# A recommendation kernel: pair products over all 128 rows, dense layers of all samples first, last tile in four units of 32 samples

## The reference, cut to what matters

```python
emb = emb_tables[arange(26)[:, None], x_cat]            # one 64-number row per sample and field
dense_embed = price[:, None] @ Wp + bp                  # a 27th row of 64
feats = concatenate([emb, dense_embed[:, None, :]], 1)  # 2048 x 27 x 64
gram = einsum('bid,bjd->bij', feats, feats)             # all pairs of the 27 rows, per sample
interactions = gram[:, _IU, _JU]                        # 351 pairs
h = relu(dense_embed @ W1 + b1)                         # 64 -> 128
dense_out = relu(h @ W2 + b2)                           # 128 -> 64
t = relu(concatenate([interactions, dense_out], 1) @ Wt1 + bt1)   # 415 -> 256
out = (t @ Wt2 + bt2)[:, 0]
```

## Time and profile before

| what | value |
|---|---|
| time, three runs | 541.97 us median (541.65 to 544.13) |
| the profiled execution | 542.15 us, its span 540.3 us |
| POOL busy | 393.8 us (73%), 416 gathers |
| PE busy | 246.3 us (46%) |
| ACT busy | 169.1 us (31%) |
| DVE busy | 145.4 us (27%) |
| mean granted TensorE clock | 0.70 |

### The profile page before, as it was taken

How to read it: one execution, slowest core, us unless ns; L and a number is a source line. 1 busy time by engine, 2 the same in 40 slices (tenths; PEclk the granted TensorE clock), 3 DMA queues, 4 the chain that set the end, 5 groups by cost and what they waited for, 6 DMA issues and landing times.

```text
span 540.3 us, 4362 instructions
## 1 busy us (share of the span) xinstructions
PE 246.3 (46%) x1496; PEld 177.9 (33%) x1496; DVE 145.4 (27%) x358; ACT 169.1 (31%) x405; POOL 393.8 (73%) x425
## 2 busy tenths in 40 slices
PE   0118033240569515134249733315136960565775
PEld 0105033240534304133234423305134440544654
DVE  3003233040331504123040331503233051333353
ACT  0124323041241604223042440503224052243563
POOL 6777777777777777777777777777777777777750
PEclk9999665555659856555577975755555985669798
DMA  6233333333323333333333333333332333332210
GB/s 187 26 26 27 26 28 27 26 27 27 26 27 27 26 27 28 26 26 27 26 29 26 27 27 26 27 27 27 26 27 26 26 28 26 26 28 27 28 22 2
DMA packets 14360, 16.26 MB, mean 30 GB/s; under 512 B 7169, under 2 KB 7425, under 8 KB 14209
## 3 DMA queue, kind: packets, MB, share of 16 engines
q0 software_dynamic: 13312, 13.66, 30.9%
q1 hardware_dynamic: 578, 2.19, 1.1%
q10 hardware_dynamic: 448, 0.14, 0.1%
HBM read 15.95 MB, written 0.01 MB: 30 GB/s over the span
## 4 chain that ended last, share of the span: by engine, by line
POOL 68%; issue 26%; DMA 2%; PE 2%; ACT 1%; DVE 0%; POOLq 0%
POOL gathered L200 68%; DMA gathered<-in_table,row_idx 2%; PE ps_mlp L487 1%; ACT gram L141 1%; PE ps_trans L419 1%; DMA raw_idx<-in_x_cat 0%; POOLq L50 0%; PE ps_gram L456 0%; PE ps_mlp L479 0%; PE ps_mlp L495 0%; DVE feats L166 0%; DVE top L368 0%; ACT scores L279 0%; DVE row_idx L339 0%; DVE wrapped L332 0%
## 5 line engine op out<-in xcount | busy, mean ns | idle before, releaser
L200 POOL DMA_INDIRECT gathered<-in_table,row_idx x416 | 392.7, 944 | 128.0 <-issue 125.9
L419 PE MATMUL ps_trans<-ident,gathered 128*128 128x128 f32 x208 | 45.4, 381 | 223.0 <-DMA gathered<-in_table,row_idx 223.0
L456 PE MATMUL ps_gram<-feats 64*128 64x128 f32 x1024 | 105.2, 384 | 61.0 <-ACT gram L141 30.2
L141 ACT COPY gram<-ps_gram 32x112 f32<-32x112 f32 (+1 forms) x272 | 97.2, 357 | 108.1 <-PE ps_gram L456 105.2
L141 DVE COPY gram<-ps_gram 32x112 f32<-32x112 f32 (+1 forms) x272 | 96.6, 355 | 116.8 <-PE ps_gram L456 113.5
L456 PEld LDWEIGHTS ps_gram<-feats 64*128 64x128 f32 x1024 | 96.9, 286 | 75.4 <-issue 52.6
L419 PEld LDWEIGHTS ps_trans<-ident,gathered 128*128 128x128 f32 x208 | 35.0, 198 | 236.3 <-issue 234.9
L151 ACT COPY feats<-ps_trans 64x448 f32<-64x448 f32 (+1 forms) x60 | 34.1, 569 | 195.4 <-PE ps_trans L419 195.0
L151 DVE COPY feats<-ps_trans 64x448 f32<-64x448 f32 (+1 forms) x60 | 36.8, 613 | 203.3 <-PE ps_trans L419 202.7
L487 PE MATMUL ps_mlp<-gram,wt1p_sb 128*128 128x512 f32 (+2 forms) x168 | 60.2, 520 | 2.9 <-ACT gram L141 2.9
L487 PEld LDWEIGHTS ps_mlp<-gram,wt1p_sb 128*128 128x128 f32 x168 | 32.6, 228 | 32.6 <-issue 28.0
(11 more groups left out here) (24 smaller groups left out, 33.5 us busy)
## 6 DMA issues: line engine op xcount, KB each, us to landing
gathered<-in_table,row_idx POOLq DMA_INDIRECT x416, 3.3
price_bc<-in_price SPq DMA_DIRECT2D x1, 1024.0 KB, 5.2
wt1p_sb<-in_wt_pairs SPq DMA_DIRECT2D x1, 896.0 KB, 7.8
raw_idx<-in_x_cat SPq DMA_DIRECT2D x1, 195.0 KB, 2.7
w_sb<-in_w ACTq DMA_DIRECT2D x2, 32.0 KB, 4.8
wt1d_sb<-in_wt_dense ACTq DMA_DIRECT2D x1, 64.0 KB, 7.7
raw_idx<-in_x_cat SPq DMA_DIRECT2D x1, 13.0 KB, 1.8
consts_sb<-in_consts ACTq DMA_DIRECT2D x1, 4.5 KB, 2.0
```

What stands on the lines that cost most here:

```text
L141: last = copy(gram_to[QUAD * c:QUAD * (c + 1), n % 2, t - BATCHES[n][0], :, rg * r:rg * (r + 1), :, s], source[QUAD * s:QUAD * (s + 1), :, ...
L200: pool.indirect_dma_start(out=gathered[:, to * D:(to + 1) * D], out_offset=None, in_=rows, in_offset=bass.IndirectOffsetOnAxis(ap=row_idx[ ...
L419: last = nc.tensor.transpose(ps_trans[:, to + k * P:to + (k + 1) * P], gathered[:, base + f * D:base + (f + 2) * D], ident[:, :])
L456: last = nc.tensor.matmul(ps_gram[:, out_at:out_at + P], group, group, start=True, stop=True)
```

## The change

Four things change.

1. Pair products of tiles 0 to 13. A new buffer `padded` is zeroed once. For each tile ACT copies the upper half of `feats` (64 partitions x 2048 numbers) into its left columns and the lower half into its right ones; the rest stays zero. One product then takes all 128 rows of four-and-four samples against 256 columns. A tile has 16 of these instead of 32.
2. The dense layers of all 2048 samples run once, ahead of tile 0, in four pieces of 512 samples; `dense_out` keeps them all.
3. The last tile is gathered in four units of 7, 6, 7 and 6 gathers, each of which brings all 26 fields of 32 samples. The row numbers for that are made by 12 small DVE additions instead of one. Tile 14 and the last tile use four rounds of 8 old-style products, over two halves of PSUM.
4. The last batch is tiles 14 and 15 together (256 samples). Its top layer runs in two parts: 224 samples after unit 2, half of it ahead of unit 3's transposes, and the last 32 samples at the end, through `ps_trans`. `WARM` is now 2, 6 and 0 products ahead of units 1, 2 and 3.

```diff
-LAST_CHUNKS = [(0, 8), (8, 16), (16, 24), (24, 26)]
-BATCHES = [(0, 4), (4, 8), (8, 12), (12, 14), (14, 15), (15, 16)]
+BATCHES = [(0, 4), (4, 8), (8, 12), (12, 14), (14, 16)]
+UNITS = 4; UNIT = P // UNITS
+EARLY = 2 * P - UNIT
-WARM = (0, 7, 3, 1, 1)
+WARM = (2, 6, 0)
...
# POOL, last tile
-            for c, (f0, f1) in enumerate(LAST_CHUNKS):
-                if c == 1:
+            pool.wait_ge(rows_made, 2 + 3 * UNITS)
+            pool.wait_ge(chunk_transposed[0], LAST)
+            for n in range(UNITS):
+                if n == 2:
                     pool.wait_ge(chunk_transposed[1], LAST)
+                for col in UNIT_COLS[n]:
+                    gather(LAST, col, unit_gathered[n])
...
# ACT
-            act.wait_ge(feats_zeroed, 1)
+            act.wait_ge(feats_zeroed, 2)
+            def pad_halves(t):
+                act.wait_ge(trans_evac_dve, NC * (t + 1))
+                act.wait_ge(trans_evac_act, NC * (t + 1))
+                act.wait_ge(dense_slot_set, 2 * (t + 1))
+                for h in range(2):
+                    nc.scalar.copy(padded[D * h:D * (h + 1), :, P * h:P * (h + 1)],
+                                   feats[D * h:D * (h + 1), :, :].rearrange("p (g s) j -> p g (s j)", s=GROUP))\
+                        .then_inc(padded_made, 1)
+            dense_batch(0)
+            for k in range(DENSE):
+                hidden_relu(k)
+                if k + 1 < DENSE:
+                    dense_batch(k + 1)
+                dense_out_relu(k)
...
# DVE, ahead of everything else
             nc.vector.memset(feats[:, :, :], 0.0).then_inc(feats_zeroed, 1)
+            nc.vector.memset(padded[:, :, :], 0.0).then_inc(feats_zeroed, 1)
...
# PE
+            def gram_round(t, r):
+                pe.wait_ge(padded_made, 2 * (t + 1))
+                wait_gram_evac(ROUNDS * t + r)
+                for g in range(RG):
+                    at = RG * r + g
+                    last = nc.tensor.matmul(ps_gram[:, 2 * P * g:2 * P * (g + 1)], feats[:, GROUP * at:GROUP * (at + 1), :],
+                                            padded[:, at, :], start=True, stop=True)
+            for k in range(DENSE):
+                hidden_layer(k)
+                dense_out_layer(k)
...
+            transpose_unit(0)
+            transpose_unit(1)
+            fine_round(LAST, 0)
+            fine_round(LAST, 1)
+            transpose_unit(2)
+            fine_round(LAST, 2)
+            top_part(0, 0)
+            transpose_unit(3)
+            fine_round(LAST, 3)
+            top_part(1, 0)
+            for m in range(2):
+                top_part(m, 1)
+            for late in range(2):
+                score_part(late)
```

More of the change, by code:

```diff
@@ L70, in rec_kernel @@
         feats = sb("feats", [P, HALF, PAD])
+        padded = sb("padded", [P, GROUPS, 2 * P])
         gram = sb("gram", [P, 2 * SLABS * WIDE * P])
@@ new lines, in dense_slots, with dense_batch @@
+                for h in range(2):
+                    part = slice(D * h, D * (h + 1))
+                    prices = price_bc[part, t * P:(t + 1) * P].rearrange("p (n h k) -> p h n k", n=UNITS, h=2)[:, h]
+                    nc.scalar.activation(feats[part, :, 0].rearrange("p (n k) -> p n k", n=UNITS), prices, ACT.Identity,
+                                         bias=const(BP, part), scale=const(WP, part)).then_inc(dense_slot_set, 1)
+            def dense_batch(k):
+                dense_features(dense[:, :], slice(0, D), k * BANK, BANK).then_inc(dense_made, 1)
@@ L280, in store_scores, with store_part @@
                                      ACT.Identity, bias=const(BT2, slice(0, 1))).then_inc(score_stored, 1)
+            def store_part(late):
+                part, _ = last_part(0, late)
+                first = BATCHES[last_batch][0] * P
+                act.wait_ge(score_summed, last_batch + 1 + late)
+                nc.scalar.activation(scores[:, first + part.start:first + part.stop],
+                                     ps_mlp[late][0:1, 0:part.stop - part.start],
+                                     ACT.Identity, bias=const(BT2, slice(0, 1))).then_inc(score_stored, 1)
@@ L317, in _ @@
-            store_scores(n)
+                for r in range(ROUNDS if t < LAST - 1 else FINE_ROUNDS):
+                    gram_round(r, t)
+            t = LAST
+            odd_unit(0)
+            dense_slots(t)
+            odd_unit(1)
+            gram_round(0, t)
+            gram_round(1, t)
+            odd_unit(2)
+            gram_round(2, t)
+            odd_unit(3)
+            part_relu(0)
+            gram_round(3, t)
+            part_relu(1)
+            store_part(0)
+            store_part(1)
@@ new lines, in top_sums @@
+            def top_sums(n, m, part, to, rounds):
+                a, first = BATCHES[n][0] * P, (n % 2) * SLABS * WIDE * P
+                nc.tensor.matmul(to, wt1d_sb[:, m * P:(m + 1) * P], dense_out[:, a + part.start:a + part.stop],
+                                 start=True, stop=False)
+                wait_gram_evac(rounds)
+                for j in range(SLABS):
+                    at = first + j * WIDE * P
+                    last = nc.tensor.matmul(to, wt1p_sb[:, j * TM1 + m * P:j * TM1 + (m + 1) * P],
+                                            gram[:, at + part.start:at + part.stop], start=False, stop=(j == SLABS - 1))
+                last.then_inc(top_summed[m], 1)
@@ L497, in score, with score_part @@
                 last.then_inc(score_summed, 1)
+            def score_part(late):
+                part, _ = last_part(0, late)
+                for m in range(2):
+                    pe.wait_ge(top_made[m], last_batch + 1 + late)
+                    last = nc.tensor.matmul(ps_mlp[late][0:1, 0:part.stop - part.start], const(WT2 + m), top[m][:, part],
+                                            start=(m == 0), stop=(m == 1))
+                last.then_inc(score_summed, 1)
+            for k in range(DENSE):
+                hidden_layer(k)
+                dense_out_layer(k)
@@ L567 @@
     idx = cat.transpose(2, 1, 0).copy()
-    idx[:, -1] = cat[:, -1].reshape(FIELDS // 2, 2, 2, UNITS, UNIT).transpose(1, 2, 4, 3, 0).reshape(P, FIELDS)
+    last = cat[:, -1].reshape(FIELDS, UNITS, 2, SIDE)
+    own = last[:SHARED].reshape(COLS, UNITS, UNITS, 2, SIDE).transpose(1, 3, 4, 2, 0).reshape(P, UNITS, COLS)
+    shared = last[SHARED:].reshape(2, 2, 2, 2, SIDE).transpose(2, 0, 3, 4, 1).reshape(P, 2)
+    for n in range(UNITS):
+        idx[:, -1, UNIT_COLS[n][0]:UNIT_COLS[n][0] + COLS] = own[:, n]
+        if n % 2 == 0:
+            idx[:, -1, UNIT_COLS[n][COLS]] = shared[:, n // 2]
     idx = idx.reshape(P, TILES * FIELDS)
```

346 lines of the change are left out of this document (170 added, 176 removed).

## The result

The changed kernel takes 545.96 us (545.18 to 546.77), the kernel before 542.01 in the same comparison: ratio 1.0074, 95% interval 1.0058 to 1.0090. Repeated later on another occasion it was 545.09 against 542.09, ratio 1.0055 (1.0035 to 1.0075). It is slower by some 3 to 4 us; the forecast was 0.6 us faster. The time lies inside the range given (538.6 to 546.0) by 0.04 us, on its slower side, to which the forecast had given 0.17.

The account below looks back on a forecast made before the run. POOL's gathers, 1.25 us each, were taken to bound the kernel. Head +0.4, between tiles 0 and tail -1.0 gave 541.5 us for the profiled execution, 541.4 predicted; range 538.6 to 546.0.

Parts of the forecast that it names:

- What bounds the kernel: Whole span: POOL issuing gathers sets the pace, 1.25 us each, never kept waiting; PE and ACT bound nothing.
- The head: Before tile 1's gathers: additions and dense layers ahead of the first transposes delay POOL; stall 0.3 us, up to 1.5.
- The 0.1 for gathers beside the additions: At the start: up to two gathers slowed by the DVE additions, 0 to 0.3 us, 0.1 taken.
- Between the tiles: TensorE's path between chunks: pad copies and longer rounds, yet POOL does not wait; 0 us.
- The three rivals there: POOL waits for TensorE, 556 (0.08); pad copies at scattered rate, 551 (0.03); pair products cost what they did, time unchanged.
- The tail: Behind the last gather, 18.4 us before: -2.7 at full clock, +0.6 with a slow stretch, -1.0 taken.
- the 15 to 19 us: Sign of error: the tail behind the last gather falling outside this range.
- all at 2.4 GHz: Tail with TensorE at full clock: -2.7 us; as a rival -2.7 to -3.3 with the head free, 538.9, chance 0.18.
- that stretch at 1.2: Tail around the first 224-column part at 1.2 GHz: part 5.6 instead of 2.9, +3.3 us, giving +0.6.
- The products of 32 columns: End of the tail: sixteen products at 0.16 us each, between 0.09 and 0.22, 2.6 us in all.
- What follows them: End of the tail: bias 0.3 us, scores and two small copies 1.3.
- both at their bad ends: Head +1.5 and tail +2, with 32 columns at 0.22 and half clock to the end: 545.5, chance 0.06.

Follow-up runs that it names:

- g_after: The changed kernel itself, unedited, run again beside its variants: 545.09 us, ratio 1.0055 to the kernel before.
- h4: Changed kernel with the last batch's top layer split at tile 14 / tile 15 and six keep-busy products moved from unit 2 to unit 3: 539.84 us, ratio 0.9959.
- h1: Changed kernel with ACT waiting for the two zeroed buffers only behind the dense layers: 544.65 us, ratio 1.0040 to the kernel before.
- h2: Changed kernel with the 64-row pair products of before in tiles 0 to 13 and no pad copies: ratio 1.0053 to the kernel before.
- h3: Changed kernel with six more keep-busy products around round 2 of the last tile: 542.31 us, ratio 1.0013 to the kernel before.
- j1: Changed kernel, zeroing wait behind dense layers, split at tile 14 / 15, keep-busy products 2 and 5 ahead of units 1 and 3: ratio 0.9956, on a chip that stands still.

## Why the prediction was wrong

**What bounds the kernel** was right: POOL's steps, 1.25 us each. The 2 ns more per step in the first profile were no part of the forecast, and g_after doesn't have them.

**The head** came out at 1.15 where 0.3 was taken and 1.5 was the bound. Each piece took 4.75 instead of 4.65, the start was 0.3 later, and POOL's gather started 0.8 us after the last transpose ended (36.72 to 37.52; 37.54 to 38.35 in h4), for which the sum has no term. h1 shows the step itself: move the one wait and the stall is gone. The 0.1 for gathers beside the additions didn't come here (0.95 us each); in h4 one took 1.27.

**Between the tiles** was right: pad copies 1.90 for 2.1, rounds of 3.7 to 6.8, chunk 0 of tile 5 at 192.9 for 191 to 194 (195.2 in g_after, POOL's gather at 199.9), no stall, and 47.5 us more of pair products on TensorE where 48 was worked out. h2 confirms that it costs no time. The three rivals there did not come.

**The tail** is the step that failed: -1.0 was forecast, +2.6 measured (21.0 against 18.4; +1.8 in g_after), outside the 15 to 19 us beyond which the prediction called itself wrong. The places were named, the sizes were off, nearly all to one side. The 3.6 us missed in the first profile:
- The clock. The middle was taken between "all at 2.4 GHz" and "that stretch at 1.2"; the second came. The part took 5.06 (2.92 at 2.4 GHz) and in this execution the round ahead of it 2.08 (1.16): with the transposes behind them some 3.1 us, where 1.7 was taken; 1.4 missed. All four profiled executions with this tail and without fillers have the part slow, at 4.42 to 5.30. h3 shows that it is the gaps.
- The products of 32 columns, 0.25 instead of 0.16, sixteen times: 1.5. The bound of 0.22 was too low as well. The sum came to it from 0.32 for 128 columns, which was read in a stretch at a clock of 0.72; at 2.4 GHz that product takes 0.26 (h4), and 32 columns cost as good as the same.
- What follows them: 1.6 was counted for bias, scores and two small copies, 2.3 measured (540.82 to 543.12); 0.7. This is the clock again: the scores' eight records took 1.86, and 1.03 in h3 at a clock of 1.00; here the clock was 0.80 from 537 to 543.

h3, at full clock all through, has a tail of -1.2 where the sum had -2.7: without the clock the sum was still too short by the 32 columns.

Weighing two ends of one's own and taking the middle hid that one of them was much likelier: the filler products of before had been moved away from just the gap in question, and that stood in the diff. The rival "both at their bad ends" (545.5, given 0.06) comes nearest to what happened, with 1.15 for its 1.5 at the head and 2.6 for its 2 in the tail. That the time of 545.96 fell inside the range is luck.

## What to carry to other kernels

When one queue sets the pace, look at what stands ahead of the last arrival in each engine's program: here a part of 5 us, more than half of whose columns had been ready since the tile before. Work split finer to shorten a tail pays only down to the size at which an instruction's time stops falling; read that from rows before cutting. And when fillers are moved, the question is which gap they leave.

## What the runs showed of the hardware

- A float32 product of 128 rows with 128 stationary columns takes 0.26 us for 128 moving columns (1.80 for seven, h4) and 0.25 for 32 (1.75 for seven, the changed kernel), in runs of seven at 2.4 GHz.
- Two products of 64 rows each on upper and lower partitions cost TensorE as little time as 0.13 us apiece, a 128-row product of 256 columns, which replaces two of them, 0.46 (3.69 for eight): padding with zeros to fill the rows nearly doubles the time, hidden here.
- TensorE's clock went down to 1.2 GHz in the changed kernel after it had worked 0.7 us of the 4.5 ahead of round 2, the longest break 2.2 us; in g_after it fell only behind that round, in h1 in the part. It stayed at 2.4 when six fillers, 3 us, were added there (h3). Under the last copies, 1.3 to 1.4 us idle with work before them, it kept 2.4 GHz without any (h4, j1).
- A gather of POOL that waited for TensorE's transposes started 0.8 us after they ended (36.72 to 37.52 in the changed kernel, 37.54 to 38.35 in h4).
- On four chips every trace stands still at each tile boundary, POOL mostly for 3 to 6 us, and the kernel before takes 655 us where it takes 542 on the others; the profile names no releaser for it.
